# First cross attention of a two-layer decoder: exponentials of each pair's second tile read from PSUM, head by head, with the negative maximum as bias

## The reference, cut to what matters

```
qh = heads(q, Wq, bq); kh = heads(k, Wk, bk); vh = heads(v, Wv, bv)      # 16 heads of 16
scores = einsum('bhsd,bhtd->bhst', qh, kh) / sqrt(16)                    # 1024 x 64 per head
scores = where(mask, scores, -1000.0)
attn = softmax(scores, axis=-1)
out = einsum('bhst,bhtd->bhsd', attn, vh); out = out @ Wo.T + bo
```

## Time and profile before

| | us |
|---|---|
| median of 3 runs | 1656.0 (1654.66 to 1659.65) |
| the profiled execution's own time | 1659.75 |
| its span, first to last instruction | 1657.5 |
| busy PE, DVE, ACT, POOL over the span | 1557.9, 943.0, 575.6, 394.5 |
| first cross attention, pairs 0 to 7 | from about 458 to 580 of the span |
| mean granted TensorE clock | 0.981 of full speed |

### The profile page before, as it was taken

How to read it: one execution, slowest core, us unless ns; L and a number is a source line. 1 busy time by engine, 2 the same in 40 slices (tenths; PEclk the granted TensorE clock), 3 DMA queues, 4 the chain that set the end, 5 groups by cost and what they waited for, 6 DMA issues and landing times. The chain is left out here.

```text
span 1657.5 us, 32015 instructions
## 1 busy us (share of the span) xinstructions
PE 1557.9 (94%) x11094; PEld 1118.6 (67%) x11095; DVE 943.0 (57%) x1719; ACT 575.6 (35%) x1135; POOL 394.5 (24%) x525
## 2 busy tenths in 40 slices
PE   7999999999989937999999999999989979999996
PEld 6744444444467726777777777866657779999995
DVE  7688888888689775112111212378878764444443
ACT  3277777777655501111111111033346510000000
POOL 2000000000022103132312111156652113333331
PEclk9999999999999959999999999999999989999998
DMA  2112221111411111123431331110024136666674
GB/s 78 39 45 67 61 59 48 43 48 43 164 33 39 52 46 49 23 89 105 108 85 33 98 92 16 23 46 1 2 86 157 52 130 186 175 177 186 184 173 115
DMA packets 89081, 134.96 MB, mean 81 GB/s; under 512 B 17568, under 2 KB 66080, under 8 KB 88832
## 3 DMA queue, kind: packets, MB, share of 16 engines
q1 hardware_dynamic: 73824, 113.05, 21.8%
q0 software_dynamic: 15168, 20.72, 7.8%
HBM read 98.00 MB, written 20.84 MB: 72 GB/s over the span
## 5 line engine op out<-in xcount | busy, mean ns | idle before, releaser
L2296 DVE TENSOR_REDUCE mx<-ps 128x1 f32<-128x1024 f32 x256 | 300.5, 1216 | 47.1 <-PE ps L2391 46.9
L1439 PE MATMUL ps<-xTe,wide 128*128 128x320 f32 x1024 | 277.4, 433 | 1.8 <-DVE hTe L1506 1.7
L1439 PEld LDWEIGHTS ps<-xTe,wide 128*128 128x128 f32 x1024 | 194.3, 190 | 82.3 <-DVE hTe L1506 2.2
L1506 DVE TENSOR_TENSOR hTe<-prT,ps 128x320 f32<-128x320 f32 x128 | 62.3, 488 | 211.2 <-ACT prT L1480 199.3
L2400 PE MATMUL ps<-QS,KS 99*128 99x512 bf16 x512 | 163.4, 380 | 0.5 <-ACT wide L2190 0.3
L2190 ACT ACTIVATE wide<-ps 128x512 f32<-128x512 f32 x256 | 137.9, 604 | 67.7 <-PE ps L2400 67.7
L2190 ACT ACTIVATE turns_of_use<-ps 128x512 f32<-128x512 f32 x256 | 135.1, 599 | 50.7 <-PE ps L2400 48.4
L2391 PE MATMUL ps<-KS,QS 96*128 96x512 bf16 x512 | 148.0, 379 | 1.0 <-DVE mx L2296 0.2
L1607 PEld LDWEIGHTS ps<-xw_all,w1t 128*128 128x128 f32 x1248 | 146.0, 193 | 2.8 <-issue 0.9
L1607 PE MATMUL ps<-xw_all,w1t 128*128 128x128 f32 x1248 | 146.4, 276 | 0.7 <-ACT xw_all L1637 0.7
L1480 ACT ACTIVATE prT<-ps 128x320 f32<-128x320 f32 x128 | 56.0, 437 | 261.9 <-PE ps L1439 255.9
(11 more groups left out here) (324 smaller groups left out, 2263.7 us busy)
## 6 DMA issues: line engine op xcount, KB each, us to landing
w1t<-in_L_ffn_w SPq DMA_DIRECT2D x39, 1024.0 KB
wide<-in_L_ffn_gate_weight SPq DMA_DIRECT2D x8, 1024.0 KB
wide<-_L_ffn_ff_pre_act_weight SPq DMA_DIRECT2D x8, 1024.0 KB
wide<-L_ffn_ff_post_act_weight SPq DMA_DIRECT2D x8, 1024.0 KB
wide<-in_L_ffn_w SPq DMA_DIRECT2D x1, 8192.0 KB, 27.5
QS<-wide SPq DMA_DIRECT2D x192, 32.0 KB, 1.9
KS<-wide SPq DMA_DIRECT2D x192, 32.0 KB, 2.0
VS<-V_all SPq DMA_DIRECT2D x32, 128.0 KB, 2.1
```

The costliest lines, as they stand in the source:

```text
L1439: ins = pe.matmul(ps[:, 3 + 2 * (q % 2) + n, 0:HC], wt[:, k, f * P:f * P + P], xTe[:, k, hf * HC:hf * HC + HC], start=(k == 0), stop=(k == ...
L1506: v.tensor_tensor(hTe[:, f, hf * HC:hf * HC + HC], sgt[:, q % 2, :], ps[:, 4 + 2 * (q % 2), 0:HC], ALU.mult).then_inc(f_m.sem, 1)
L2296: v.tensor_reduce(mx[:, s, t:t + 1], ps[:, 2 * (t % 2):2 * (t % 2) + 2, :], AX.XY, ALU.max).then_inc(h_rm.sem, 1)
```

## The change

For layer 0 and the second tile of each pair (`j = 1`) DVE no longer subtracts. It writes the negative of the 16 maxima into a small tile `nmx` (128 x 16) and signals that. ACT reads the masked scores in banks 0 and 1 directly, in 16 instructions of 64 columns, one for each head, each with that head's column of `nmx` as the bias of the exponential, and writes `pr[:, 1, h, :]`. The last of the 16 signals `x_e`. The wait for PE having turned the last pair's `pr[:, 1]` moves with it from DVE to ACT. Because ACT is now the last reader of banks 0 and 1, `pe_scores` of a pair's first tile also waits for `x_e` of the pair before (up to and with the first pair of layer 1). First tiles, and all of layer 1, stay as they were.

```diff
+        nmx = sbX("nmx", [P, H])
@@
             def probs(U, j):
                 act.wait_ge(x_sm.sem, x_sm.upto(U, j + 1))
-                act.activation(pr[:, j, :, :], pr[:, j, :, :], ACT.Exp).then_inc(x_e.sem, 1)
+                if (layer, j) == (0, 1):
+                    act.wait_ge(x_pt.sem, x_pt.upto(U - 1))
+                    S2 = ps[:, 0:2, :].rearrange("p r (h k) -> p (r h) k", k=SC)
+                    for h in range(H):
+                        ins = act.activation(pr[:, 1, h, :], S2[:, h, :], ACT.Exp, bias=nmx[:, h:h + 1])
+                    ins.then_inc(x_e.sem, 1)
+                else:
+                    act.activation(pr[:, j, :, :], pr[:, j, :, :], ACT.Exp).then_inc(x_e.sem, 1)
@@ def softmax
+                if (layer, j) == (0, 1):
+                    v.tensor_scalar(nmx[:], mxx[:, 1, :], -1.0, None, ALU.mult).then_inc(x_sm.sem, 1)
+                    return
                 v.wait_ge(x_pt.sem, x_pt.upto(U - 1, 2 * j + 2))
                 v.tensor_tensor(pr[:, j, :, :], S2, mxx[:, j, :].unsqueeze(2).to_broadcast([P, H, SC]),
                                 ALU.subtract).then_inc(x_sm.sem, 1)
@@ def pe_scores
             pe.wait_ge(x_sm.sem, x_sm.upto(U, j))
+            if j == 0 and U <= NP:
+                pe.wait_ge(x_e.sem, x_e.upto(U - 1))
```

## The result

The changed kernel takes 1688.2 us (median of 4 runs, 1684.1 to 1692.6) against 1657.1 us (4 runs), a ratio of 1.0185 with a 95% interval of 1.0164 to 1.0207: 31 us slower, where 27 had been forecast. The profiled execution took 1688.85 us with a span of 1687.0, against 1659.75 and 1657.5.

What follows compares the result with a forecast made beforehand. PE was taken to set the pace, with ACT's second-tile exponential right beside its step between pairs. Profiled 1659.75 + 21.2 (waits) + 6 (clock) = 1687 us; the median being 3.75 lower, forecast 1683, range 1674 to 1695.

Steps and rivals of the forecast that it cites:

- What bounds: First cross attention: PE sets the pace, busy 13.94 of 14.37 us a pair; ACT's second-tile exponential ends it without cover.
- The price of the set: ACT, second tile: 16 exponentials of 64 columns take 15 x 0.21 + 0.31 = 3.46 us, instead of one of 1.05.
- my upper bound of 3.97: ACT's 16 exponentials: a step of 0.242 us by line 1827, 15 x 0.242 + 0.34 = 3.97 us.
- The crossings: PE's step between pairs waits for ACT's last exponential: 3.36, 2.63, five of 2.78, and 1.35 in pair 7; 21.2 us.
- the 0.25 that I had named: PE's wait for DVE's first-tile softmax before the turn: at most 0.25 us could come back in each pair.
- Nothing made good later: Output, routing and experts follow the last pair, each behind the one before, so all 21.2 us of delay reach the end.
- The clock: PE's new gaps, 2.7 us a pair and 4.3 at pair 0, lower its clock after about half of eight: 6 us.
- a fall costs 1.67: PE's clock dropping to 0.50 after a gap: 1.67 us each if PE is loaded throughout, taken at 1.5.
- The rival without falls: PE waits for ACT but its clock holds: 1656 + 21 = 1677 us; chance 0.22.
- The rival with a dearer step: ACT's step is 0.24 us, PE's gap 3.2, and the clock falls nearly each time: 36.5 us more, 1692; chance 0.15.

Runs made afterwards that it cites:

- The set of 16 in SBUF: Kernel before, second tile's exponential cut into 16 of 64 columns in SBUF; DVE still subtracts, PE's scores don't wait for ACT: 1692.4 us against 1659.6, ratio 1.0191.
- the run with the clock held: Changed kernel plus filler matmuls in PE's gaps (17 at first crossing, 10 at others, 8 more before pair 7's last turn): 1676.2 us against 1658.2, ratio 1.0111.

## Why the prediction was right

- *What bounds.* Right: PE, with ACT's second exponential beside its last step. The run with the wait alone put the old slack to the test: 3.0 us expected, 3.0 measured.
- *The price of the set.* Built from line 616 at 3.46, measured 3.39, but by two terms whose errors nearly cancel. I had a step of 0.21 and one exponential at 0.31, with 0.10 of overlap; the group below has a mean of 0.372, which leaves (3.39 - 0.37)/15 = 0.20 for the step and 0.17 for the overlap. The set of 16 in SBUF took 3.92, by the second row with a step of (3.92 - 0.34)/15 = 0.24, and there my upper bound of 3.97, from the SBUF rows at line 1827, would have been close. The fixed cost of an instruction, 0.15, is three times its 64 columns (0.05), not four. The Trainium skill (ScalarE: Activation LUTs, What ACT_TABLE_LOAD costs) gave 3.93 as an estimate; the set in SBUF agrees with it, at 3.92, and the set out of PSUM is 14% under it, so here the measurement decides.

```profile
L627 ACT ACTIVATE pr<-ps,nmx 128x64 f32<-128x64 f32 x128 | 27.1, 372 | 1.3 <-DVE nmx L765 1.3
```

```profile
L624 ACT ACTIVATE pr<-pr,zeros 128x64 f32<-128x64 f32 x128 | 31.4, 338 | 2.2 <-DVE pr L762 2.2
```

- *The crossings.* Forecast 3.36, 2.63, five of 2.78 and 1.35, together 21.2. In the run with the clock held: 3.38, 2.64, 2.48, four of 2.78 and 1.27, together 20.9. The 0.3 of the third is a wait of PE for DVE in pair 2 that went away, of the size of the 0.25 that I had named as the most that could come back; in full pairs a wait of 0.24 for DVE stayed. Both hang on the first tile, and why only the one went away was not traced.
- *Nothing made good later.* Right in the main: the routing's first maximum starts 30.3 us later in the profile and the span is 29.5 longer. What lies between, 1.8 us taken back and 1.4 lost, is of the size that the other runs show at the same places.
- *The clock.* Right in kind, and the term that was mis-sized. I took a fall at about half of eight gaps, so four at 1.5 us, 6 us. That share was a guess, and it was luck that the profiled execution had just four. In pairs 1, 3 and 7 they cost 18.64 - 15.86 = 2.8, 21.27 - 17.15 = 4.1 and 14.86 - 13.48 = 1.4 (the second number of each from the run with the clock held), and the fourth, behind the stage, 1.7 (from the last turn to the routing are 18.5 us, where before and with the clock held they are 16.8). That is 10. The price that I read off the fillers, 1.67, was that of one slow stretch of 3.4 us, and the two falls with stretches of 3.4 cost 1.4 and 1.7. The other two stayed at 0.50 for 6.8 and 10.3 us. The step that failed is "a fall costs 1.67": it took for granted how long a fall lasts.
- *The sum.* 1656 + 21.2 + 6 = 1683; by the measured terms 20.9 + 10 = 31, and 1688.2 - 1657.1 = 31. That they agree so closely is in part chance, since the changed kernel's four executions lie 8.5 us apart. The lower end of the range, 1674, is 3 us under the rival's 1677 and not 2.

The rival without falls (1677, 21 over before) is near what the run with all gaps filled shows, 1676 and 18 over the kernel before beside it. The rival with a dearer step took its falls at nearly one in each pair, and had the total closest; but its step, 0.24, was wrong for this source.

## What to carry to other kernels

Ask of an engine that looks idle whether the step you lengthen has another engine right behind it: ACT had 40% of idle time and none at that place. When one instruction is cut into many to fit a value to each group, count the fixed cost of each (0.15 us here, against 0.05 for its columns), and look first for one value that serves all groups. And a new gap of PE is to be priced twice, by its length and by the clock behind it; if it can't be removed, fillers that fit inside it give the second part back.

## What the runs showed of the hardware

The clock did not go by the length of a gap alone: of five gaps of 2.71 to 2.72 us two were followed by a stretch at 0.50 and three were not; with 5.1 us in each pair every one came with such a stretch, and with 1.50 still two of five. How long it then stays low also varies, 3.4 to 10.3 us in the changed kernel, at much the same load, and up to 13.7 in the run with 32 instructions. What else decides was not settled. A slow clock did not always cost time: in the routing it was at 0.50 for 41.0 us in the kernel before and for 44.4 in the changed one, with PE busy for about 40% of that, and from the routing's first maximum on DVE (585.78 and 616.13) to PE's matmuls behind its fillers (632.47 and 662.82) are 46.69 us in both.

In a row of 16 an exponential of 64 columns with a bias from a column took a step of 0.20 us out of PSUM and 0.24 out of SBUF, 3.39 and 3.92 for the set. Moving the work into one instruction is worth more: 1024 columns then took 1.11 us out of PSUM with a bias from a column, and 1.05 out of SBUF without one.
